# Expert outputs weighted and added by an accumulating indirect DMA to one row per token, in place of two stored rows per token

## The reference

```
x = x + L0_gnn(layernorm(x))     three GraphSAGE layers
x = x + L0_ffn(layernorm(x))     mixture of 8 experts, 2 per node
x = x + L1_gnn(layernorm(x))     sum of h[src] + relvectors[rel] over the edges, then a GRU cell
x = x + L1_ffn(layernorm(x))     mixture of 16 experts, 2 per node, then a layernorm inside
```

## Time and profile before

| what | value |
|---|---|
| time, three runs | 1780.93 us median, 1779.05 to 1782.27 |
| profiled execution | 1773.84 us, span 1772.1 us |
| PE busy | 1473.6 us, 83% |
| DVE busy | 871.9 us, 49% |
| ACT busy | 481.6 us, 27% |
| POOL busy | 336.9 us, 19% |
| memory read, written | 103.12 MB, 57.93 MB |
| first expert stage | from about 820 to 1040 us |
| relate, part before the remaining sums | about 1040 to 1115 us |
| second expert stage | from about 1444 to 1703 us |
| combine | about 1703 to 1769 us |

### The profile page before, as it was taken

How to read it: one execution, slowest core, us unless ns; L and a number is a source line. 1 busy time by engine, 2 the same in 40 slices (tenths; PEclk the granted TensorE clock), 3 DMA queues, 4 the chain that set the end, 5 groups by cost and what they waited for, 6 DMA issues and landing times. The chain is left out here.

```text
span 1772.1 us, 34488 instructions
## 1 busy us (share of the span) xinstructions
PE 1473.6 (83%) x8498; PEld 1031.8 (58%) x8499; DVE 871.9 (49%) x2496; ACT 481.6 (27%) x1231; POOL 336.9 (19%) x391
## 2 busy tenths in 40 slices
PE   4795989989998999975999956998998649999920
PEld 3674744457443855534898932444665638899820
DVE  6996833323222357774222248312888452222258
ACT  2564400012000311112444433001222414444421
POOL 3000210012000300002554420000000514555420
PEclk9555999999999999986999979998999559999965
DMA  4000321123111422222223257202221334332444
GB/s 122 0 0 12 107 75 47 47 75 119 51 50 47 127 91 83 83 76 85 92 95 127 100 155 234 90 24 74 69 67 42 107 134 155 115 115 92 132 129 129
DMA packets 134622, 158.41 MB, mean 89 GB/s; under 512 B 16929, under 2 KB 119698, under 8 KB 134258
## 3 DMA queue, kind: packets, MB, share of 16 engines
q1 hardware_dynamic: 122642, 125.59, 22.4%
q0 software_dynamic: 11840, 32.12, 6.0%
q10 hardware_dynamic: 96, 0.20, 0.0%
HBM read 103.12 MB, written 57.93 MB: 91 GB/s over the span
## 5 line engine op out<-in xcount | busy, mean ns | idle before, releaser
L875 PE MATMUL agg_ps<-parts,counts 128*128 128x512 f16 x1875 | 410.5, 380 | 8.7 <-PEq L653 8.0
L875 PEld LDWEIGHTS agg_ps<-parts,counts 128*128 (+1 forms) x1875 | 183.6, 98 | 227.6 <-issue 13.5
L1441 ACT ACTIVATE experts_hT<-experts_ps_h,experts_b_col 128x128 f32<-128x128 f32 x456 | 165.8, 367 | 186.4 <-PE experts_ps_h L1416 161.1
L1424 PE MATMUL experts_ps_y<-experts_rows,experts_hT 128*128 128x256 f32 x688 | 163.0, 380 | 0.0
L1379 POOL DMA_INDIRECT chosen<-experts_y,experts_row x116 | 114.6, 988 | 146.6 <-issue 107.9
L1368 POOL DMA_INDIRECT experts_fetched<-tokens,experts_index x120 | 116.1, 967 | 93.9 <-ACT experts_x L1445 41.0
L777 POOL TENSOR_TENSOR parts<-proj_rest,gru_rows 128x256 f32 (+2 forms) x75 | 54.4, 726 | 416.8 <-DVE proj_rest L755 416.8
L1424 PEld LDWEIGHTS experts_ps_y<-experts_rows,experts_hT 128*128 128x128 f32 x688 | 124.3, 191 | 13.4
L1416 PE MATMUL experts_ps_h<-experts_xT,experts_rows 128*128 128x128 f32 x976 | 122.1, 279 | 8.9 <-issue 7.8
L1416 PEld LDWEIGHTS experts_ps_h<-experts_xT,experts_rows 128*128 128x128 f32 x976 | 118.9, 194 | 17.5 <-issue 13.8
L1465 DVE COPY experts_xT<-experts_ps_x 128x256 f32<-128x256 f32 x114 | 48.4, 425 | 162.4 <-PE experts_ps_x L1405 162.4
(11 more groups left out here) (314 smaller groups left out, 2039.5 us busy)
## 6 DMA issues: line engine op xcount, KB each, us to landing
experts_rows<-in_L_ffn_w SPq DMA_DIRECT2D x32, 512.0 KB, 4.8
gru_rows<-x SPq DMA_DIRECT2D x75, 128.0 KB, 2.2
own<-proj_own SPq DMA_DIRECT2D x75, 128.0 KB, 1.7
gru_rows<-own SPq DMA_DIRECT2D x75, 128.0 KB, 2.1
h<-agg_out SPq DMA_DIRECT2D x50, 128.0 KB, 1.7
gru_rows<-h SPq DMA_DIRECT2D x50, 128.0 KB, 2.0
gru_rows<-chosen SPq DMA_DIRECT2D x50, 128.0 KB, 2.3
combine_y<-chosen SPq DMA_DIRECT2D x50, 128.0 KB, 2.1
```

Source lines behind the costliest of these rows:

```text
L875: last = nc.tensor.matmul(ps[b][:], cst.counts[:, s, bass.ds(t * P, P)], parts[:, s, :], start=s == 0, stop=s == NT - 1)
L1424: last = nc.tensor.matmul(ps_y[:, 0:D], hT[:, c, :], down[b][:, c, :], start=c == 0, stop=c == KH - 1)
L1441: nc.scalar.activation(hT[:, c, :], ps_h[c][:, 0:P], function, bias=b1_col[:, bass.ds(e * KH + c, 1)]).then_inc(hT_ready, 1)
```

## The change

Each expert's output row is multiplied by its weight before it is stored, and the store becomes an indirect DMA that adds to its destination row. The destination is `dr.x1` in the first mixture (the rows of the first block lie there already) and a new tensor `dr.mixed` in the second, which `score_rows` fills with the token rows. `dr.chosen`, `dr.x2` and `plan.weight` go.

- Token rows get two more columns in memory: `dr.tokens` has rows of 258 values, so a row is 1032 bytes and no longer 1024. The two weights of a token lie in the last two columns. `route` computes them earlier in DVE's stream (right behind the logits' gap) and SP stores them in one DMA of 3200 runs of 8 bytes, behind its loads of the first experts. POOL waits for that store before the first fetch.
- In `run_experts` a fetch brings the weights along; two small DVE instructions per tile pick the right one (`weigh`), and DVE multiplies the 128x256 output tile by it. PE may overwrite the product's bank once b2 is added (`y_taken`), before the multiplication.
- `relate` loads one tile per step and neither adds nor stores x2; its four buffers hold the rows until they are normalised. `combine` becomes `finish`, which loads one tile per step and adds nothing.
- `score_rows` stores each tile twice. `gru` reads `dr.x1`. Two DMAs of zeros are added to the first stage.

The core of the diff:

```
@@ build_counts, sync
-                sp.wait_ge(filled, 16 * 2)
+                for total in (dr.x1, dr.mixed):
+                    sp.dma_start(total[NP:NP + P, :], zeros[:]).then_inc(filled, 16)
+                sp.wait_ge(filled, 16 * 4)
@@ score_rows, sync
-                    sp.dma_start(dr.tokens[rows(t), :], tile_of(tokens, t)).then_inc(stored, 16)
+                    sp.dma_start(dr.tokens[rows(t), 0:D], tile_of(tokens, t)).then_inc(stored, 16)
+                    sp.dma_start(dr.mixed[rows(t), :], tile_of(tokens, t)).then_inc(stored, 16)
@@ route, sync
+                sp.wait_ge(weights_ready, 1)
+                sp.dma_start(dr.tokens[:, D:D + 2].rearrange("(t p) c -> p t c", p=P), weight[:]).then_inc(weights_stored, 16)
@@ route, vector (behind L1184)
+                dve.wait_ge(exp_ready, 1)
+                nc.vector.tensor_scalar(least[:], ratio[:], 1.0, None, ALU.add)
+                dve.drain()
+                nc.vector.reciprocal(weight[:, :, 0], least[:])
+                dve.drain()
+                nc.vector.tensor_tensor(weight[:, :, 1], weight[:, :, 0], ratio[:], ALU.mult).then_inc(weights_ready, 1)
@@ route, vector (L1236 to L1258)
-                (the same three instructions, into plan.weight)
-                nc.vector.tensor_scalar(second, ps_token[1][:, 0:MT], 0.0, float(NP), ALU.not_equal, ALU.mult)
+                nc.vector.tensor_scalar(plan.second[:], ps_token[1][:, 0:MT], 0.0, None, ALU.not_equal)
+                nc.vector.tensor_scalar(plan.first[:], ps_token[1][:, 0:MT], 0.0, None, ALU.is_equal)
...
@@ route, gpsimd
+                pool.wait_ge(weights_stored, 16)
                 pool.wait_ge(token_ready, 1)
@@ open_experts
-    weights.fetched, ... = sb("fetched", [P, 2, D]), ...
+    weights.fetched, ... = sb("fetched", [P, 2, D + 2]), ...
@@ run_experts, gpsimd
-                    pool.indirect_dma_start(dr.chosen, bass.IndirectOffsetOnAxis(ap=row[:, b:b + 1], axis=0), y[:, b, :],
-                                            None).then_inc(y_stored, 16)
+                    pool.indirect_dma_start(total_rows, bass.IndirectOffsetOnAxis(ap=row[:, b:b + 1], axis=0), y[:, b, :],
+                                            None, compute_op=ALU.add).then_inc(y_stored, 16)
@@ run_experts, tensor
-                        pe.wait_ge(y_ready, q + 1)
+                        pe.wait_ge(y_taken, q + 1)
@@ run_experts, vector
+                def weigh(q, b):
+                    pair = fetched[:, bass.ds(b, 1), D:D + 2].rearrange("p a d -> p (a d)")
+                    nc.vector.tensor_tensor(part[:, 0:1], pair[:, 1:2], plan.second[:, bass.ds(q, 1)], ALU.mult)
+                    dve.drain()
+                    return nc.vector.scalar_tensor_tensor(weight[:, bass.ds(q, 1)], pair[:, 0:1], plan.first[:, bass.ds(q, 1)],
+                                                          part[:, 0:1], ALU.mult, ALU.add)
...
-                        nc.vector.tensor_copy(index[...], plan.token[...]).then_inc(index_ready, 1)
+                        nc.vector.tensor_copy(index[...], plan.token[...])
+                        weigh(q + 2, q % 2).then_inc(index_ready, 1)
...
-                        nc.vector.tensor_tensor(y[...], ps_y[:, 0:D], b2_all[...], ALU.add).then_inc(y_ready, 1)
+                        nc.vector.tensor_tensor(mine, ps_y[:, 0:D], b2_all[...], ALU.add).then_inc(y_taken, 1)
+                        dve.drain()
+                        nc.vector.tensor_scalar(mine, mine, weight[:, bass.ds(q, 1)], None, ALU.mult).then_inc(y_ready, 1)
@@ relate, sync
                     sp.dma_start(x[b], dr.x1[rows(t), :]).then_inc(got[b], 16)
-                    for c in range(2):
-                        sp.dma_start(y[b][c], dr.chosen[bass.ds(c * NP + t * P, P), :]).then_inc(got[b], 16)
...
-                    sp.wait_ge(taken, t + 1)
+                    store_normed(t, b)
                     if not past(t + B):
                         load(t + B, b)
-                    sp.dma_start(dr.x2[rows(t), :], out[b % 2][:]).then_inc(stored[b % 2], 16)
-                    if not early(t - 1):
-                        store_normed(t - 1, b + 1)
@@ relate, vector, one step
-                    dve.wait_ge(got[b], k * 48 + 48)
-                    scalar_tensor_tensor(mixed[d], y[b][0], plan.weight[0][t], x[b], mult, add)
+                    dve.wait_ge(got[b], k * 16 + 16)
+                    bn_stats(small[d][:, 0:6], x[b])
                     if behind:
                         inverse_of(t - 1, before_d)
                     if not early(t - 2):
-                        dve.wait_ge(stored[d], use * 16)
-                    dve.wait_ge(begun, t + 1)
-                    scalar_tensor_tensor(out[d], y[b][1], plan.weight[1][t], mixed[d], mult, add)
+                        remain(t - 2, d)
                     if behind:
                         dve.wait_ge(inverted, t)
-                        norm_of(t - 1, before_use, before_d)
-                    dve.wait_ge(taken, t + 1)
-                    bn_stats(small[d][:, 0:6], out[d])
-                    if not early(t - 2):
-                        remain(t - 2, d)
+                        norm_of(t - 1, before_use, before_d, b - 1)
                     dve.drain()
                     bn_aggr(small[d][:, 6:8], small[d][:, 0:6])
@@ combine -> finish, vector, one step
-                    scalar_tensor_tensor(mixed[d], y[b][0], plan.weight[0][t], tile_of(tokens, t), mult, add)
+                    bn_stats(small[d][:, 0:6], mixed[b])
                     if behind:
                         inverse_of(t - 1, before_d)
-                        norm_of(t - 1, before_d)
-                    scalar_tensor_tensor(mixed[d], y[b][1], plan.weight[1][t], mixed[d], mult, add)
+                        norm_of(t - 1, before_d, b - 1)
+                    dve.drain()
+                    bn_aggr(small[d][:, 6:8], small[d][:, 0:6])
                     if behind:
                         last_of(t - 1, before_use, before_d)
-                    bn_stats(small[d][:, 0:6], mixed[d])
-                    dve.drain()
-                    bn_aggr(small[d][:, 6:8], small[d][:, 0:6])
```

More of the change, by code:

```diff
@@ L1290, in open_experts @@
     weights.b1, weights.b1_rows, weights.b1_loaded = b1, sb("b1_rows", [experts * KH, P]), sem("b1_loaded")
-    weights.fetched, weights.fetch_done = sb("fetched", [P, 2, D]), [sem(f"fetch_done{b}") for b in range(2)]
+    weights.fetched, weights.fetch_done = sb("fetched", [P, 2, D + 2]), [sem(f"fetch_done{b}") for b in range(2)]
     weights.loaded = [sem(f"w_loaded{b}") for b in range(buffers)]
@@ L1301, in load_expert, with run_experts @@
         weights.loaded[b], 16)
-def run_experts(nc, cst, dr, tag, weights, b2, function, plan):
+def run_experts(nc, cst, dr, tag, weights, b2, function, plan, total_rows):
     with ExitStack() as ctx:
@@ L1320, in run_experts @@
         y = sb("y", [P, 2, D])
+        part, weight = sb("part", [P, 2]), sb("weight", [P, plan.token.shape[1]])
         ps_x, ps_y, ps_b = pb("ps_x", [P, KD, P]), pb("ps_y", [P, BANK]), pb("ps_b", [P, BANK])
@@ L1482, in _, with relate @@
                 dve.sem_inc(x_ready, 1)
-def relate(nc, ins, cst, dr, plan, parts, w_rows):
+def relate(nc, ins, cst, dr, parts, w_rows):
     rels = slice(REL_ROW, REL_ROW + N_REL)
@@ L1498, in relate @@
         B = 4
-        y = [[w_rows[:, c, b, :] for c in range(2)] for b in range(B)]
-        x = [w_rows[:, b // 2, B + b % 2, :] for b in range(B)]
-        mixed, out, small = pair("mixed", [P, D]), pair("out", [P, D]), pair("small", [P, 10])
+        x = [w_rows[:, 0, b, :] for b in range(B)]
+        total, red, small = pair("total", [P, D]), pair("red", [P, D]), pair("small", [P, 10])
         hn, rest = pair("hn", [P, D]), pair("rest", [P, D])
@@ L1706, in _, with finish @@
                 sums_loop(dve, keep_sums)
-def combine(nc, cst, dr, tag, plan, tokens, base, gamma, output):
+def finish(nc, cst, dr, tag, base, gamma, output):
     with ExitStack() as ctx:
@@ L1717, in combine @@
         B = 4
-        y = [[sb(f"y{b}_{c}", [P, D]) for c in range(2)] for b in range(B)]
-        mixed, out, small = pair("mixed", [P, D]), pair("out", [P, D]), pair("small", [P, 10])
+        mixed = [sb(f"mixed{b}", [P, D]) for b in range(B)]
+        out, small = pair("out", [P, D]), pair("small", [P, 10])
         normal, scale, w_loaded = pair("normal", [P, D]), sb("gamma", [P, D]), sem("w_loaded")
@@ L2005, in four_blocks @@
     dr = Scratch()
-    dr.x0, dr.x1, dr.x2 = (scratch(f"x{i}", NP) for i in range(3))
+    dr.x0, dr.x1, dr.mixed = scratch("x0", NP), scratch("x1", NP + P), scratch("mixed", NP + P)
     dr.h1, dr.h2 = scratch("h1", NP), scratch("h2", NP)
@@ L2043, in plan_for @@
                 plan = Plan()
-                plan.weight = [pb(f"weight{c}", [P, NT]) for c in range(2)]
                 plan.bounds = pb("bounds", [1, experts, 2], I32)
```

(5 more changed lines are left out.)

117 lines of the change are left out of this document (48 added, 69 removed).

## The result

The change makes the kernel slower: 1869.68 us median of 4 runs (1864.95 to 1874.64) against 1779.99 us (1778.43 to 1782.27), a ratio of 1.0503, 95% interval 1.0473 to 1.0533. The profiled execution took 1869.7 us with a span of 1868.0 us, 95.9 us more than the 1772.1 us of before. The forecast was 1810 us: right in sign, too small by some 60 us, and the result lies above its own range of 1787 to 1861 us.

The account below looks back on a forecast made before the run. PE was taken to bound the expert stages, DVE and DMA relate and combine. Costs of +68 us, +62.0 of them stores, less 39 gave +29: 1803 us, 1810 on the median's scale; own range 1787 to 1861, 8 in 10 1752 to 1890.

Parts of the forecast that it names:

- The bound now: Expert stages: PE bounds at 3.73 us per tile; POOL's serial stores, 3.465 us apart, have 0.265 us of slack.
- The accumulating store: Expert stages: an adding store lands 0.75 us later than a plain one, bounds 0 and 2.0; interval 4.215 us.
- The term of POOL: POOL's store instruction, 0.987 us: a third descriptor per row to make, put at 0.1 us.
- The forecast's own case: Expert stages: the store chain binds, extra landing 0.55 to 1.2 us; 1810 us, from 1787 to 1861; chance 0.50.
- 1.2 and above: Adding store: load then store in series, or rows one by one; 1955 us at 2.0 us extra landing; chance 0.14.
- The rival of a nearly free accumulate: Adding store: the second read shares a mostly fixed latency; 0.3 us extra landing gives 1758 us; chance 0.30.
- The other end: Adding store: a whole load in front of each store, 2.0 us extra landing, 1955 us; in the 0.14 band.
- The sum of the stores: Both expert stages: 114 intervals of 4.215 us plus 25.3 us for expert loads, 505.8 us against 443.8, a loss of 62.0.
- The price of a load: Expert stages: each of 6 and 12 expert loads disturbs the stores by 1.4 us, 25.3 us together.
- Smaller terms: Outside the store intervals: weights 1.6 us, instruction before `plan.token` 0.4, weights' store 2, `score_rows` 0.5; fetched rows and zeros nothing.
- Relate and combine: Relate falls from 2.70 to 1.95 us per tile, combine from 2.38 to 1.58; together 39 us gained.
- The signs to look for: Profile after: landing near 3.2 us, stores 4.2 apart, DVE's row-number copy ended by POOL, PE waiting for DVE.

Follow-up runs that it names:

- two half-row runs: The changed kernel storing only the first 128 columns of each output row (64 KB): with the adding 1799.89 us, ratio 1.0165; without it 1739.74 us.

## Why the prediction was right in sign and wrong in size

**The bound now** was read rightly: a serial chain of stores with 0.265 us of slack per tile. The forecast rested on it, and it held: the interval is landing plus 1.06 us before and after, and with 4.87 us, above PE's 3.73, PE starves. The way by which it starves was read wrongly. The prediction has DVE wait for a free buffer (`y_free`) at its copy of the row number; that copy (L1489) stood idle for 11.3 us in all, and hardly for POOL. DVE waits for 251.8 us one step earlier, at L1485, and ACT for 344.2 us at L1451, both for POOL's word that the next rows have been fetched, which POOL gives only behind the store. By the program both words hang on the same landing, so the price per tile is the same, but the remedy isn't: in the kernel with two stores in flight, moving POOL's word ahead of its wait gained 23 us.

**The accumulating store: here is the error.** The step took d = 0.75 us as 0.2 for reading memory, 0.44 for bytes and 0.1 for POOL's descriptors; it measured 1.4. The runs with 64 KB split it: the extra landing of an adding store is 3.3 - 2.2 = 1.1 us at 64 KB and 1.4 at 128 KB, so 0.3 us for each 64 KB and 1.4 - 2 x 0.3 = 0.8 us that don't depend on bytes. POOL's instruction alone is 0.6 us longer, which leaves 0.2. By the prediction's own terms: reading memory 0.2 (0.2), bytes 0.6 (0.44), POOL 0.6 (0.1). The intervals between stores are finer than the landings and say nearly the same: 4.87 - 3.50 = 1.37 us at 128 KB and 4.36 - 3.33 = 1.03 at 64, so 0.68 for bytes, 0.60 for POOL and 0.1 left. The term of POOL was put at 0.1 because a third descriptor for each of 128 rows seemed little beside 0.987 us. It was the one term with no row behind it, and the time moves by 114 us for each us of it. That POOL's 0.6 us lie in series with the landing fits the sums, but no run took them away alone. The queue's share of the 16 DMA engines bears on it, 11.0% in after and in the run without the adding:

```profile
q0 software_dynamic: 11840, 32.25, 6.3%
```

Spread evenly over the 16 engines (an estimate), that is (0.110 x 1868.0 - 0.063 x 1741.5) / 116 = 0.83 us more per store at 128 KB, and with the 8.1% and 5.1% of the two half-row runs (0.081 x 1796.6 - 0.051 x 1738.0) / 114 = 0.50 at 64 KB. With POOL's 0.60 us in series that makes 1.43 and 1.10 us, and 1.4 and 1.1 were measured: two sums that agree, and no proof.

The forecast's own case ended at d = 1.2 (1861 us). The measured 1.4 lies in the band "1.2 and above" that was given 0.14, but not by that band's mechanism.

The rule of the Trainium skill (DMA: Bandwidth & Descriptors, "Anatomy of one DMA"), a fixed part of some 2 us and bytes over 436 GB/s, made the second 128 KB an estimated 0.3 us; the trace disagrees, with 0.6 us for these bytes and 1.4 us in all. The rival of a nearly free accumulate, 1758 us, is refuted. The other end, two full latencies in series (d = 2.0, 1955 us), is refuted too.

**The sum of the stores** was 480.5 + 25.3 = 505.8 us, and is 567.6. With d = 1.4 the same formula gives 114 x 4.865 = 554.6; the 18 loads then have 13.0 us, 0.7 each, not 1.4. So d was worth +74 us and the loads -12: the whole miss of 62 us in this term, smaller by luck, since two errors went opposite ways. The 13.0 us are a remainder and no measurement of the loads; an error of 0.05 us in d would move it by 6 us. The price of a load had come from one pair of intervals.

**Smaller terms.** From `plan.token` to the first store it is 6.5 us longer over both stages: 3.5 us in the first (14.01 to 17.50) and 3.0 in the second. The prediction had 1.6 for the weights and 2 for the store of the weights. Nothing of that store is exposed: it lands 6.6 us after its issue at 804.23 in the first stage and 9.5 us after that at 1467.2 in the second, long before the first fetches of 823.54 and 1489.62. In the first stage the 3.5 us are three pieces: from `plan.token` to POOL's fetch 1.1 us for 0.5; from there to DVE's copy of x 829.66 - 823.54 = 6.1 us for 4.5, 0.4 of it the two weighing instructions; from there to the store 10.3 us for 9.0, with the multiplication in it. That the fetch itself came 1.2 us later wasn't foreseen, and whether its longer rows are the cause stays open. The store of token rows, whose rows now lie 1032 bytes apart, lands after 2.2 us instead of 1.7 and is hidden:

```profile
tokens<-tokens SPq DMA_DIRECT2D x25, 128.0 KB, 2.2
```

The last landings add 1.4 us each. Of the rest of the 95.9 us, 3.1 us were there before the first route begins (last use of `agg_out` at 786.0 instead of 782.9), and are no effect of the change, since the run without the adding has the same code up to there and stands at 781.9. Together that is 123.8 + 6.5 + 2.8 + 3.1 - 39.0 = 97.2 us, 1.3 more than measured.

**Relate and combine** were right: 1.94 us per tile for 1.95, 18.4 us for 18; 1.52 for 1.58, 20.6 us for 20. The loop between ACT and DVE is there, and not only its interval: from 1112 to 1156 ACT waits for DVE's normalisation 23 times (24.2 us) and DVE for ACT's root 20 times (8.8 us), while PE, which was to be late next and was busy 47.52 of the 52 us, waits for ACT for 0.5 us.

**The signs to look for**: landing near 3.2 us was said and is 3.8, stores 4.2 apart are 4.87; the DVE wait in front of PE is there (46.3 us), the POOL wait in front of DVE too, but at the token number and not at the row number that was named. A line that wasn't foreseen is ACT's copy of x with 344.2 us of waiting for POOL (61.3 before): the fetch, called hidden by two tiles of lead, is hidden only as long as POOL isn't waiting for a store.

## What to carry to other kernels

Before a plain store becomes an adding one, ask how many are in series: here 1.4 us on each of 114 intervals outweighed 39 us saved elsewhere, while the same adding stores with two in flight beat the kernel before by 0.6%. Find out where the data really conflict (only between experts) and hold only there; and in an in-order stream put every message that others need ahead of any wait that they don't need. A term of a prediction that has no row behind it needs its own range, however small it looks.

## What the runs showed of the hardware

- An indirect store with an add takes POOL 1.59 us where a plain one takes 0.99. It depends little on rows (1.435 us at 64 of 128) and not on bytes (1.586 us at half a row).
- It lands after 3.8 us for 128 x 1 KB (plain: 2.4), 3.3 for 128 x 512 bytes, 3.2 for 64 x 1 KB. Bytes cost 0.5 us per 64 KB, against 0.2 plain (worked out from intervals).
- Adding takes the queue from 11840 packets to 22976 for the same 32.25 MB, and from 6.3% of the 16 engines to 11.0%.
- Whether the token rows it adds to are shared between stores or not makes no difference (both 3.8 us).
- Beside 1 MB of loads an adding store's landing was up to 6.4 us.
- Rows written at a distance of 1032 bytes instead of 1024 land after 2.2 us instead of 1.7.
